# Keys and values projected by plain fp32 products in a Perceiver layer: no splits, eight context buffers, values out on ScalarE

## What is computed

```
q = layernorm(x) @ Wq.T + bq            # 128 x 256, 16 heads of 16
k = ctx @ Wk.T + bk                     # 12544 x 256
v = ctx @ Wv.T + bv                     # 12544 x 256
scores = (q * 0.25) . k  for each head  # 16 x 128 x 12544
ctx_out = softmax(scores) @ v           # 128 x 256
x1 = x + ctx_out @ Wo.T + bo
x2 = x1 + linear_attention(layernorm(x1))      # exp/identity feature map, sigmoid gate
y  = x2 + block(layernorm(x2))                 # RoPE attention, then top-2 of 8 experts
```

## Time and profile before

| | us |
|---|---|
| median of the 3 runs | 576.75 |
| the 3 runs | 576.61, 576.75, 581.04 |
| span of the profiled execution, first to last instruction | 577.4 |
| TensorE matmul busy in it | 544.8 (94%) |
| VectorE busy | 421.6 (73%) |
| ScalarE busy | 330.7 (57%) |
| GpSimd busy | 92.1 (16%) |

### The profile page before, as it was taken

How to read it: one execution, slowest core, us unless ns; L and a number is a source line. 1 busy time by engine, 2 the same in 40 slices (tenths; PEclk the granted TensorE clock), 3 DMA queues, 4 the chain that set the end, 5 groups by cost and what they waited for, 6 DMA issues and landing times.

```text
span 577.4 us, 15741 instructions
## 1 busy us (share of the span) xinstructions
PE 544.8 (94%) x6460; PEld 502.4 (87%) x6460; DVE 421.6 (73%) x797; ACT 330.7 (57%) x635; POOL 92.1 (16%) x75
## 2 busy tenths in 40 slices
PE   7888989999999999999999999999998998778897
PEld 7777989999999999999999999999987877736686
DVE  5689868778777787787787877877877317866674
ACT  3423747667676676675666766766764850062463
POOL 7641101011011011110110111101000000015000
PEclk9999999999999999999999999999999999978899
DMA  6999995856977878777678787796575019920000
GB/s 196 152 158 152 182 154 97 120 119 120 129 120 115 128 121 124 118 113 129 119 114 128 121 122 118 120 125 101 78 118 175 3 38 377 375 87 1 1 1 9
DMA packets 44615, 70.41 MB, mean 122 GB/s; under 512 B 6784, under 2 KB 15104, under 8 KB 44416
## 3 DMA queue, kind: packets, MB, share of 16 engines
q1 hardware_dynamic: 44304, 69.02, 65.8%
q10 hardware_dynamic: 240, 0.39, 0.5%
HBM read 30.53 MB, written 0.13 MB: 53 GB/s over the span
## 4 chain that ended last, share of the span: by engine, by line
PE 80%; DVE 8%; DMA 6%; SPq 2%; ACT 1%; issue 1%; POOL 0%; DVEq 0%
PE bank L608 17%; PE bank L624 15%; PE bank L584 14%; PE bank L567 10%; PE bank L556 10%; DMA kT<-kst 5%; PE bank L834 3%; PE bank L850 3%; SPq L244 2%; PE bank L632 2%; DVE stepmax L946 1%; DMA qmat<-maxT 1%; PE bank L654 1%; PE bank L532 1%; PE bank L647 1%
## 5 line engine op out<-in xcount | busy, mean ns | idle before, releaser
L946 DVE TENSOR_REDUCE stepmax<-bank 128x2 f32<-128x512 f32 x392 | 262.9, 688 | 92.2 <-PE bank L584 68.7
L403 ACT ACTIVATE probs<-bank 128x512 f32<-128x512 f32 x392 | 229.8, 601 | 139.8 <-PE bank L608 135.6
L608 PE MATMUL bank<-qmat,kT 128*128 128x256 f32 x784 | 164.5, 294 | 4.2 <-DMA kT<-kst 3.4
L584 PE MATMUL bank<-kT,qM 128*128 128x256 f32 x784 | 161.2, 287 | 4.1 <-DVE stepmax L946 1.9
L608 PEld LDWEIGHTS bank<-qmat,kT 128*128 128x128 f32 x784 | 120.8, 191 | 18.9 <-issue 9.9
L584 PEld LDWEIGHTS bank<-kT,qM 128*128 128x128 f32 x784 | 121.5, 191 | 7.7 <-DVE stepmax L946 4.0
L316 POOL TENSOR_TENSOR cparts<-ctxT,cparts 128x512 fp32r<-128x512 f32 x49 | 63.4, 1294 | 326.7 <-ACT cparts L363 326.6
L556 PE MATMUL bank<-cparts,wk 128*128 128x256 f32 x588 | 101.3, 283 | 2.1 <-POOL cparts L316 2.1
L567 PE MATMUL bank<-wv,cparts 128*128 128x256 f32 x588 | 101.9, 284 | 0.7 <-ACT val L383 0.7
L624 PE MATMUL bank<-probs,val 128*17 128x128 f32 x3136 | 95.1, 273 | 0.0
L624 PEld LDWEIGHTS bank<-probs,val 128*17 128x17 f32 x3136 | 81.4, 97 | 6.5
(11 more groups left out here) (188 smaller groups left out, 320.7 us busy)
## 6 DMA issues: line engine op xcount, KB each, us to landing
kT<-kst SPq DMA_DIRECT2D x291, 128.0 KB, 4.6
ctxT<-in_ctxT SPq DMA_DIRECT2D x49, 256.0 KB, 5.5
w<-in_w SPq DMA_DIRECT2D x24, 512.0 KB, 10.0
bias<-in_biases SPq DMA_DIRECT2D x1, 1024.0 KB, 7.3
kT<-kst ACTq DMA_DIRECT2D x3, 128.0 KB, 5.0
qmat<-maxT SPq DMA_DIRECT2D x24, 8.0 KB
w_xk<-in_w_xk SPq DMA_DIRECT2D x1, 256.0 KB, 3.1
w_xq<-in_w_xq SPq DMA_DIRECT2D x1, 256.0 KB, 3.6
```

Source lines behind the costliest of these rows:

```text
L403: act.activation(probs[k % PROBS][:, :, :], sc_bank[k % 3][:, :].rearrange("p (h q) -> p h q", q=P), ACT.Exp).then_inc(S["exp_ready"], 1)
L584: last = pe.matmul(mx_bank[p % 2][:, a * SK:(a + 1) * SK], qM[:, p, a, :], kT[:, n % RING, p, :], start=True, stop=True)
L608: last = pe.matmul(sc_bank[k % 3][:, i * 2 * P:(i + 1) * 2 * P], kT[:, n % RING, p, j * P:(j + 1) * P], qmat[b % 2][:, p, :, :], start=Tru ...
L946: dve.tensor_reduce(stepmax[:, n - first_step(block_of(n)), 2 * p:2 * p + 2], mx_bank[p % 2][:, :].rearrange("p (a k) -> p a k", a=2), AX_ ...
```

## The change

The high and low parts of context and weights go, with the two engines' work on them (`context_high`, `context_low`, the two weight splits, the tiles `cparts`, `wk`, `wv`) and their semaphores. `keys` and `values` multiply the loaded tiles in plain fp32, one product for each half: 8 in a step. They wait for the load of the context piece itself. `ctxT` has eight buffers, and a load waits until the keys and values of the piece eight earlier are projected. The loads' places in SyncE's program stay; the loop now issues the loads of pieces 4 to 7 with no wait for a buffer. `values_out` runs on ScalarE for every piece, in the place (q = 5) where `context_high` stood. GpSimd keeps `key_ones` and `queries` alone in its loop. Three of the gap fillers in the tail are changed: 6 identity products become 16 over 32 rows each, 7 become 8 of 64 rows and 256 columns in fp32r, and 6 become 10 of 64 rows and 128 columns in fp32r. Some tiles move in SBUF.

```diff
-CRING = 4
+CRING = 8
...
         ctxT = [place(f"ctxT{i}", [P, DC, SK]) for i in range(CRING)]
-        cparts = [place(f"cparts{i}", [P, 2, DC, SK], F32R) for i in range(2)]
-        wk = place("wk", [P, 2, DC, D], F32R)
-        wv = place("wv", [P, 2, DC, D], F32R)
+        w = {n: place("w_" + n, [P, DC, D]) for n in ("xk", "xv")}
...
             def ctx_load(n):
 
                 if n >= CRING:
-                    sp.wait_ge(S["cl_ready"], n - CRING + 1)
+                    sp.wait_ge(S["k_done"], n - CRING + 1)
+                    sp.wait_ge(S["v_done"], 2 * (n - CRING) + 2)
...
-            for n in range(2, CRING):
+            for n in range(2, 4):
                 ctx_load(n)
             for t in range(-2, NS + 1):
-                if CRING <= t + 6 < NS:
+                if t + 6 < NS:
                     ctx_load(t + 6)
...
             key_ones(0)
-            context_low(0)
             key_ones(1)
             for t in range(-2, NS):
-                if t + 3 < NS:
-                    context_low(t + 3)
                 if 2 <= t + 4 < RING:
                     key_ones(t + 4)
...
-            act.wait_ge(S["ld_k"], 32)
-            act.activation(wk[:, 0, :, :], w["xk"][:, :, :], ACT.Copy).then_inc(S["act_wkvh"], 1)
-            context_high(0)
             act.wait_ge(S["ld_const"], 16)
             act.activation(ident_r[:, :], ident, ACT.Copy).then_inc(S["act_ident"], 1)
             keys_high(0)
-            context_high(1)
-            act.wait_ge(S["ld_v"], 16)
-            act.activation(wv[:, 0, :, :], w["xv"][:, :, :], ACT.Copy).then_inc(S["act_wkvh"], 1)
             first_keys_half()
...
-                    if q == 5 and t + 2 <= LAG:
+                    if q == 5 and t + 2 < NS:
                         values_out(t + 2)
-                    if q == 5 and t + 4 < NS:
-                        context_high(t + 4)
...
+            def context_loaded(n):
+
+                pe.wait_ge(S[f"ld_ctx{n % CRING}"], 16 * (n // CRING) + 16)
...
-                for i in range(3 * half, 3 * half + 3):
-                    pw, pc, c = products[i]
-                    if (n, t, i) == (0, 0, 4):
-                        pe.wait_ge(S["cl_ready"], 1)
-                    last = pe.matmul(k_bank[:, t * SK:(t + 1) * SK], wk[:, pw, c, t * P:(t + 1) * P], cparts[n % 2][:, pc, c, :],
-                                     start=(i == 0), stop=(i == 5))
+                last = pe.matmul(k_bank[:, t * SK:(t + 1) * SK], w["xk"][:, half, t * P:(t + 1) * P],
+                                 ctxT[n % CRING][:, half, :], start=(half == 0), stop=(half == DC - 1))
...
-                for i in range(3 * half, 3 * half + 3):
-                    pw, pc, c = products[i]
-                    last = pe.matmul(v_bank[:, j * D:(j + 1) * D], cparts[n % 2][:, pc, c, j * P:(j + 1) * P], wv[:, pw, c, :],
-                                     start=(i == 0), stop=(i == 5))
+                last = pe.matmul(v_bank[:, j * D:(j + 1) * D], ctxT[n % CRING][:, half, j * P:(j + 1) * P],
+                                 w["xv"][:, half, :], start=(half == 0), stop=(half == DC - 1))
...
                     if p == 2 and a == 1 and n + 3 < NS:
-                        pe.wait_ge(S["cl_ready"], n + 4)
+                        context_loaded(n + 3)
...
+            def keep_busy_rows(n):
+
+                for i in range(n):
+                    r = slice(32 * (i % 4), 32 * (i % 4) + 32)
+                    pe.matmul(B[4 + i % 4][:, 0:P], ident[r, :], ident[r, :], start=True, stop=True)
+
+            def keep_busy_halves(n, wide):
+
+                for i in range(n):
+                    r = slice(64 * (i % 2), 64 * (i % 2) + 64)
+                    if wide:
+                        pe.matmul(B[6 + i % 2][:, 0:2 * P], ident_r[r, :],
+                                  ident_r[r, :].unsqueeze(1).broadcast_to([64, 2, P]), start=True, stop=True)
+                    else:
+                        pe.matmul(B[6 + i % 2][:, 0:P], ident_r[r, :], ident_r[r, :], start=True, stop=True)
...
             project(xnT, ["xo"], B[1]).then_inc(S["pe_xo"], 1)
 
 
-            keep_busy(6)
+            keep_busy_rows(16)
             pe.wait_ge(S["dve_a_xn"], 1)
...
             last.then_inc(S["pe_a_num"], 1)
-            keep_busy(7)
+            keep_busy_halves(8, True)
             pe.wait_ge(S["dve_a_out"], 1)
...
-            keep_busy(6)
+            keep_busy_halves(10, False)
             pe.wait_ge(S["dve_c_xn"], 1)
...
-            def values_out(n):
-
-
-                dve.wait_ge(S["v_done"], 2 * n + 2)
-                if n >= VRING:
-                    dve.wait_ge(S["pv_done"], 2 * (n - VRING) + 2)
-                dve.tensor_copy(val[:, n % VRING, :, :, 0:HD].rearrange("p j h d -> p (j h) d"),
-                                v_bank[:, :].rearrange("p (g d) -> p g d", d=HD)).then_inc(S["val_ready"], 1)
...
                     if q == 5 and LAG < t + 2 < NS:
                         values_out(t + 2)
```

More of the change, by code:

```diff
@@ L61 @@
 COUNTING = [
-    "ch_ready",
-    "cl_ready",
     "k_done",
@@ L87 @@
 ONCE = [
-    "pool_setup", "act_ident", "dve_pvzero", "dve_warm", "act_wkvh", "dve_wkvl",
+    "pool_setup", "act_ident", "dve_pvzero", "dve_warm",
     "dve_xn", "pe_xnT", "dve_xnT", "pe_q", "dve_qparts", "pe_qT", "dve_q0", "act_q0",
@@ L100 @@
 ]
-LOADS = ["ld_x", "ld_const", "ld_q", "ld_k", "ld_v", "ld_ctx0", "ld_ctx1", "ld_ctx2", "ld_ctx3", "ld_small", "ld_tail",
+LOADS = ["ld_x", "ld_const", "ld_q", "ld_k", "ld_v", "ld_ctx0", "ld_ctx1", "ld_ctx2", "ld_ctx3", "ld_ctx4", "ld_ctx5", "ld_ctx6", "ld_ctx7",
+         "ld_small", "ld_tail",
          "ld_experts0", "ld_experts1", "ld_experts2", "ld_experts3", "experts_loaded", "stored"]
@@ L165, in perceiver_layer @@
         at[0] = parts_start
-        w = {n: place("w_" + n, [P, DC, D]) for n in ("xk", "xv", "xq")}
+        w["xq"] = place("w_xq", [P, DC, D])
         qparts = place("qparts", [P, PAIRS, 2, 4, HD], F32R)
@@ L173, in perceiver_layer @@
             w[n] = place("w_" + n, [P, DC, D])
-        assert at[0] <= temps_start
+        tail_weights_end = at[0]
+        assert tail_weights_end <= parts_start
         at[0] = arena_start
@@ L187, in perceiver_layer @@
         assert at[0] <= tail_start
-        at[0] = temps_start
+        at[0] = tail_weights_end
         ta = place("ta", [P, 2 * D])
@@ L312, in _ @@
         def _(pool):
[L313 to L318, removed]
             def key_ones(r):
@@ L357, in _ @@
         def _(act):
[L358 to L364, removed]
             def keys_high(n):
                 act.wait_ge(S["k_done"], n + 1)
+                if n == 0:
+                    act.wait_ge(S["ld_k"], 32)
                 if n >= 2:
@@ L429, in _ @@
             values_out(0)
-            context_high(2)
             values_out(1)
-            context_high(3)
             for t in range(LAST + 2):
@@ L534, in project @@
                 return last
-            products = [(pw, pc, c) for pw, pc in ((0, 0), (1, 0), (0, 1)) for c in range(DC)]
+            def context_loaded(n):
+                pe.wait_ge(S[f"ld_ctx{n % CRING}"], 16 * (n // CRING) + 16)
             def keys(n, t, half):
                 if (t, half) == (0, 0):
[L542 to L545, removed]
+                    if n < 3:
+                        context_loaded(n)
                     if n >= 1:
@@ L661, in _ @@
             warm_up(6)
-            pe.wait_ge(S["dve_wkvl"], 1)
+            pe.wait_ge(S["ld_k"], 32)
             for t in range(2):
@@ L679, in _ @@
                 last.then_inc(S["pe_qT"], 1)
-            pe.wait_ge(S["dve_wkvl"], 2)
+            pe.wait_ge(S["ld_v"], 16)
             for n in range(2):
@@ L977, in _ @@
             layernorm(xn[:, :], x[:, :]).then_inc(S["dve_xn"], 1)
-            dve.wait_ge(S["act_wkvh"], 1)
-            dve.tensor_tensor(wk[:, 1, :, :], w["xk"][:, :, :], wk[:, 0, :, :].bitcast(F32), ALU.subtract
-                              ).then_inc(S["dve_wkvl"], 1)
             turned(xnT, B[4], "pe_xnT", "dve_xnT")
@@ L992, in _ @@
                                      ALU.mult, ALU.subtract).then_inc(S["dve_qparts"], 1)
-            dve.wait_ge(S["act_wkvh"], 2)
-            dve.tensor_tensor(wv[:, 1, :, :], w["xv"][:, :, :], wv[:, 0, :, :].bitcast(F32), ALU.subtract
-                              ).then_inc(S["dve_wkvl"], 1)
             dve.wait_ge(S["pe_qT"], 1)
@@ L1014, in _ @@
                                 max_turned(b)
-                    if q == 5 and LAG < t + 2 < NS:
-                        values_out(t + 2)
             dve.wait_ge(S["ld_small"], 64)
```

## The result

Measured: 602.0 us, the median of 594.99, 606.52, 597.49 and 606.51, against 576.68 before on the same chip. The profiled execution is the one of 594.99, with a span of 593.2.

The account below looks back on a forecast made before the run. TensorE was taken to bound the long middle. Projections +23.5, softened waits -1.0, start -0.9, tail +1.8 gave +23.4 on the 576.75 median: 600.2 us, own range 598 to 603.5, wider range 595 to 605.

Parts of the forecast that it names:

- TensorE bounds the middle, and work taken from the others gives nothing: Long middle, 92 to 418 us: TensorE busy all 8.78 us of a step; relieving ScalarE, VectorE, GpSimd saves 0.
- A product costs 0.432, a stripe 0.072 more, a step 9.36: Projections: one two-pass fp32 product replaces three fp32r (0.36); step 8.78 to 9.36, 22.0 us over steps 8 to 45.
- The issue-switch rival, B: Projections: each change between fp32r and fp32 costs 0.05 us, 0.4 a step, +16 in all, so 616; chance 0.06.
- Softened waits, -1.0: Block ends in the middle: a longer step hides part of 2.7 us of waits; 0 to -2, taken as -1.0.
- Steps 5 and 6 +1.2, step 46 +0.3, steps 0 to 4 nothing: Projections outside the middle: TensorE-bound steps 5, 6 and 46 lengthen; in steps 0 to 4 key placing hides the extra.
- The start, -0.9: Start: GpSimd's fills close up, the second query copy stretches less, keys 2 start earlier; 0 to -1.7, taken as -0.9.
- The row filler, +1.8: Tail's first filler: 32 row passes at 0.112 take 3.6 us, ending 1.8 late; if passes overlap, 0.
- The clock, 0 with 2 us either way: Tail: where the shifted tail meets TensorE's clock falls to 0.50 can't be told; 0, with 2 us either way.
- rival C: Softened: DMA waits give -2, the start -1.7, row fillers overlap at 0; +19.8, so 596.5; chance 0.13.

Follow-up runs that it names:

- The values alone: Kernel before with only the values projected by plain fp32 products, keys keeping three fp32r products, six context buffers: 586.85 us, ratio 1.017.
- the fills apart: Changed kernel with GpSimd's second fill of ones waiting for VectorE's normalized rows: 597.02 us, ratio 1.035 to the kernel before.
- the old fillers: Changed kernel with the three tail gap fillers of the kernel before put back: 603.22 us, ratio 1.045 to the kernel before.
- the kernel with one product: Kernel before with only the high x high fp32r product for keys and values, low-part corrections left out: 547.36 us, ratio 0.949.

## Why the prediction was right, and where it was not

The forecast of 600.2 lies 1.8 from the measured 602.0, inside its own range, and slower is right. By its steps:

*TensorE bounds the middle, and work taken from the others gives nothing.* Right. VectorE at 68% and GpSimd at 5% left the step at TensorE's 9.32, and moving the values back changed nothing. GpSimd's busy time fell by the 63 us foreseen, VectorE's by 19 and not by 29: a step's window fell by 0.49 us for a copy listed at 0.680, since busy time counts overlapping records once.

*A product costs 0.432, a stripe 0.072 more, a step 9.36.* Right in kind, the added time of a stripe 7% too large: 0.427, 0.067, 9.32. Why twelve passes back to back in the tail gave 0.005 more a product is open. Over 38 steps that is 20.5 for 22.0. The values alone at 9.05 show that it goes by products.

*The issue-switch rival, B:* fell with that step; 0.427 between fp32r products is no more than 0.432 among fp32 ones, so nothing is left over for a change of form.

*Softened waits, -1.0.* 355.29 - 38 x 9.32 = 1.1 against 2.7 before: -1.6, inside the bounds.

*Steps 5 and 6 +1.2, step 46 +0.3, steps 0 to 4 nothing.* The sum is right where the held operation is absent: with the fills apart the weighted values of step 8 start at 83.40 for 83.15, +0.3, as forecast for this leg. Inside it the steps are not right. SyncE's queue, the placings for steps 1 to 3, before:

```profile
18.29 4.72 SPq L244 DMA_DIRECT2D kT<-kst  x6
24.41 3.75 SPq L244 DMA_DIRECT2D kT<-kst  x6
30.48 4.12 SPq L244 DMA_DIRECT2D kT<-kst  x6
```

and with the fills apart:

```profile
17.00 3.87 SPq L243 DMA_DIRECT2D kT<-kst  x6
23.63 4.53 SPq L243 DMA_DIRECT2D kT<-kst  x6
31.14 3.76 SPq L243 DMA_DIRECT2D kT<-kst  x6
```

1.3 us are won at the first of them by the shorter query copy, and lost again, with 0.7 more, by the third. On the chain the landing got longer, 8.11 us from 20.27 where it had been 6.87 from 27.56; what makes it longer wasn't tried. On the other side the wait for keys ahead of step 8 went (18.64 for 19.70), which gives 1.1 back. Two errors cancelled.

*The start, -0.9.* This step failed. "With no low parts between them GpSimd's fills run one after another from 3.3 us and the fifth ends at about 12.4" was right (12.28), and I took from it only what ceases: the stretched query copy, which did shrink, from 2.68 us to 0.49. I had the row that shows VectorE's SBUF copy held to the end of a fill and did not ask which VectorE operation now falls into the fills. It is the one ahead of all of TensorE's real work at the start. Held to the second fill it costs 0.8 us at the first keys; held to the fifth, step 6 and all behind it stand 7.7 later still. That is what sets the two groups of times apart; with up to 4.7 us of difference in the tail on top they come close to each other (the held execution of the old fillers, with a short tail, took 602.49). The Trainium skill bears on this: "SBUF — State Buffer" says of the port pair that VectorE and GpSimd share that it is an exclusive lock, held for the whole instruction, and that the other engine's operation "fully blocks", for VectorE operations in a two-port mode, which it says a tensor_scalar can enter. The trace agrees for one fill (0.41 becomes 1.30). That a waiting VectorE operation can be held on through the fills behind, for 6.69 us, it does not say. The rows of the experiments show the hold, and that it ends with the row of fills; how it passes from fill to fill they do not show.

*The row filler, +1.8.* Failed; "if passes over different rows overlap" was the true end, and it costs 0. Of the two statements of the Trainium skill in "TensorE: Matmul & The Clock Gate", the one in "LDWEIGHTS (loading the stationary operand)", that a load of 32 rows takes as long as one of 128, holds for a single load (186 ns on average against 192 in the trace after), but 32 of them overlap to 0.98 us in all. By Part 3's row tiling the estimate was 1.2, and 1.17 was measured.

*The clock, 0 with 2 us either way.* Too narrow. What follows the end of the last weighted values took 99.4 to 99.5 us in three of eleven profiles, 102.2 in three and 103.8 to 104.1 in five (the kernel with one product left out). The tail's length goes with the time that the clock is low in it: 6.8 us in the first three, 13.7 in the next three, 17.1 in the last five. The groups don't follow the kernel: the changed one had 99.4 once and 102.2 once. The profile before has 104.1 and the one after 99.4, so 4.7 us between these two say nothing on the change.

So the middle carries +18.9 in each profile of the changed kernel, and an execution held to the second fill has 1.5 + 18.9 + 0.1 = 20.5 over before with an equal tail: 597.2, near rival C (596.5) and in part by C's reasons. The median came to my 600.2 and beyond because, by their times, half of the executions or more carry 8 us that no step of mine contained. That the number fell into my range was luck in this part: it was better than its working.

## What to carry to other kernels

When a change takes work out of an engine, look at what now closes up behind it, not only at what ends earlier: list the operations of the engine it shares SBUF with that fall into the closed row, above all those on the way to TensorE's first work. Where TensorE is the bound, as here, three fp32r products of 256 columns (0.36 us) are cheaper than one plain fp32 product (0.427), and the split's work on the other engines cost nothing in the middle. And before two profiles are subtracted, compare their clock rows: here the tail alone differed by up to 4.7 us between executions of like programs.

## What was not expected of the hardware

A VectorE operation from SBUF to SBUF of 128x256 fp32 (0.41 us alone) that became ready during memsets of GpSimd, 1.8 us each and back to back, was held by them: 1.30, 3.07 and 6.69 us long, to about 0.15 us after the end of the second, third and fifth. With five in a row the same program did either the first or the last of these. VectorE's small operations on statistics (128x1) ran beside the same memsets in 0.14 to 0.27 us.

After 6.0 us without work for TensorE early in the program the granted clock was at its lower level for 6.8 us, although TensorE was busy for most of them; after 1.68 us without work it stayed at the upper level.

Thirty-two passes with weights of 32 rows and 128 columns, on four groups of rows in turn, took 1.17 us together, where twelve with 128 rows took 1.50.

The same tail of small dependent operations took 99.4, 102.2 or about 104 us, with the clock at its lower level for 6.8, 13.7 or 17.1 us of it, in no relation to the kernel.
